# Reciprocal roots of the head norms: GpSimd's power in place of VectorE's Newton steps, in a four-layer conditioned transformer

## The reference, cut to what matters

```python
def _L0_cond_ref(x, c, ...):                     # 16 heads of 18 features
    xn = _ln(x) * (1 + sc_msa) + sh_msa
    q, k, v = heads(xn @ w_qkv + b_qkv)
    q = _ln(q, g_q); k = _ln(k, g_k)             # (q - m) * rsqrt(mean((q - m)**2) + 1e-6) * g
    attn = softmax(q @ k.T * HD ** -0.5)
    x = x + g_msa * ((attn @ v) @ w_proj + b_proj)
    xn2 = _ln(x) * (1 + sc_mlp) + sh_mlp
    return x + g_mlp * (gelu(xn2 @ w1 + b1) @ w2 + b2)
# layer 1: the same without the norms of q and k
# layer 2: the norms of q and k with gain and bias, eps 1e-5
# after it: x + ((x U) R - x U) U^T, R the exponential of a skew matrix made from the condition
```

## Time and profile before

| | us |
|---|---|
| median of 2 runs (4815.79 and 4824.53) | 4820.16 |
| the profiled execution's own time | 4821.86 |
| its span, first to last instruction | 4820.1 |
| PE busy | 4250.8 (88%) |
| DVE busy | 3660.6 (76%) |
| ScalarE busy | 2302.1 (48%) |
| GpSimd busy | 1114.8 (23%) |
| mean granted TensorE clock | 0.943 of full |

### The profile page before, as it was taken

How to read it: one execution, slowest core, us unless ns; L and a number is a source line. 1 busy time by engine, 2 the same in 40 slices (tenths; PEclk the granted TensorE clock), 3 DMA queues, 4 the chain that set the end, 5 groups by cost and what they waited for, 6 DMA issues and landing times. The chain is left out here.

```text
span 4820.1 us, 124616 instructions
## 1 busy us (share of the span) xinstructions
PE 4250.8 (88%) x46073; PEld 3595.5 (75%) x46073; DVE 3660.6 (76%) x7659; ACT 2302.1 (48%) x3894; POOL 1114.8 (23%) x2045
## 2 busy tenths in 40 slices
PE   6754899999999977999999999949989989898998
PEld 4543788888888865888888888737777777777776
DVE  5665889999888845777777777658778787877874
ACT  1212555555555534555555555435454444545443
POOL 1002222222222222222222222212222222222211
PEclk7576999999999988999999999979999999999998
DMA  3001111111111111111111111110010100001000
GB/s 76 21 0 52 32 29 29 29 29 29 29 29 29 27 54 30 30 29 29 29 29 29 29 29 29 37 43 24 20 30 20 28 21 28 21 20 30 20 26 18
DMA packets 122230, 141.59 MB, mean 29 GB/s; under 512 B 14446, under 2 KB 117780, under 8 KB 122112
## 3 DMA queue, kind: packets, MB, share of 16 engines
q1 hardware_dynamic: 121968, 139.75, 10.6%
q10 hardware_dynamic: 144, 0.22, 0.0%
HBM read 110.87 MB, written 29.06 MB: 29 GB/s over the span
## 5 line engine op out<-in xcount | busy, mean ns | idle before, releaser
L869 DVE TENSOR_REDUCE mx<-S 128x4 f32<-128x1024 f32 x768 | 902.7, 1217 | 190.3 <-PE S L1105 187.4
L627 ACT ACTIVATE pT<-S 128x1024 f32<-128x1024 f32 x768 | 745.3, 1023 | 363.2 <-PE S L1133 358.9
L575 ACT ACTIVATE hf<-M 128x512 f32<-128x512 f32 (+1 forms) x480 | 266.2, 555 | 841.8 <-DVE hl L860 597.1
L504 POOL TENSOR_SCALAR hh<-hf 128x512 fp32r<-128x512 f32 (+1 forms) x480 | 286.8, 602 | 1037.2 <-ACT hf L575 1016.4
L1133 PE MATMUL S<-qT,kT 32*128 32x256 f32 x9216 | 427.3, 296 | 65.6 <-ACT pT L627 62.8
L1146 PE MATMUL A<-pT,V 128*32 128x256 f32 x6144 | 416.0, 389 | 26.6 <-ACT pT L627 26.6
L1133 PEld LDWEIGHTS S<-qT,kT 32*128 32x128 f32 x9216 | 330.3, 186 | 138.8 <-ACT pT L627 90.3
L1185 PE MATMUL M<-xh,w_hi 128*128 128x256 f32 x1728 | 365.9, 293 | 3.5 <-POOL xh L480 3.5
L1224 PE MATMUL M<-w_lo,hh 128*128 128x288 f32 x1728 | 351.6, 304 | 0.0
L1185 PE MATMUL M<-xh,w_lo 128*128 128x256 f32 x1728 | 345.0, 281 | 0.0
L1185 PE MATMUL M<-xl,w_hi 128*128 128x256 f32 x1728 | 341.1, 281 | 0.2 <-DVE xm L792 0.2
(11 more groups left out here) (231 smaller groups left out, 9800.8 us busy)
## 6 DMA issues: line engine op xcount, KB each, us to landing
mid<-xbo SPq DMA_DIRECT2D x64, 288.0 KB, 3.2
xld<-mid SPq DMA_DIRECT2D x64, 288.0 KB, 3.0
xa<-mid SPq DMA_DIRECT2D x64, 288.0 KB, 3.6
gA<-gates SPq DMA_DIRECT2D x96, 144.0 KB, 3.3
gM<-gates SPq DMA_DIRECT2D x96, 144.0 KB, 3.0
xld<-in_x_dram SPq DMA_DIRECT2D x32, 288.0 KB, 3.5
xa<-in_x_dram SPq DMA_DIRECT2D x32, 288.0 KB, 3.5
out_dram<-xbo SPq DMA_DIRECT2D x32, 288.0 KB, 2.2
```

The lines of the kernel that those rows point to most:

```text
L504: pool.tensor_scalar(hh[:, 2 * f:2 * f + m, :].rearrange("p m c -> p (m c)"), hf[:, f % 2, 0:m * T], 1.0, 0.0, ALU.mult, ALU.add).then_inc ...
L575: act.activation(hf[:, f % 2, 0:c], MBANK[f % 2][:, 0:c], ACT.Gelu if rot else ACT.Gelu_apprx_tanh).then_inc(s["m_hf"], 1)
L627: act.activation(pT[:, g % 2, 2 * h:2 * h + 2, :], S[:, 2 * h:2 * h + 2, :], ACT.Exp, scale=float(HD) ** -0.5).then_inc(s["a_ex"], 1)
L869: dve.tensor_reduce(mx[:, p, :, :], S[:, r:r + 2, :].rearrange("p a (t k) -> p a t k", t=NT), AX.X, ALU.max).then_inc(s["a_mx"], 1)
```

## The change: what it does

GpSimd gets a new function, `A_heads_rstd`, after the reciprocal root of the layer norm of `nxt` and before the rounding `A_xh`. It waits for the head sums (`a_hs`), makes the mean plus eps in `na` (semaphore `a_hv`) and raises it to -0.5 into `ny` (semaphore `a_hr`). DVE's function of that name, its twelve instructions and their call go; `A_heads_norm` on DVE now first waits for `a_hr`. `mhalf` holds -0.5 and is broadcast along the columns.

```diff
-    a_sq=1, a_hs=1, a_nrm=1, a_v=2, ...
+    a_sq=1, a_hs=1, a_hv=1, a_hr=1, a_nrm=1, a_v=2, ...
...
+                    def A_heads_rstd(n):
+
+                        wait(pool, "a_hs", qk_run(n), 1)
+                        constant_wait(pool)
+                        pool.tensor_scalar(na[:, :], nv[:, :], 1.0 / HD, eps, ALU.mult, ALU.add).then_inc(s["a_hv"], 1)
+                        wait(pool, "a_hv", qk_run(n), 1)
+                        pool.tensor_tensor(ny[:, :], na[:, :], mhalf[:, 0:1].broadcast_to([P, 64]), ALU.pow).then_inc(s["a_hr"], 1)
...
                         if nxt is not None:
                             A_rstd(nxt)
+                        if p is not None and eps is not None:
+                            A_heads_rstd(p)
+                        if nxt is not None:
                             A_xh(nxt)
...
-                    STEPS_P = 0 if eps is None else 14 if rot else 13
+                    STEPS_P = 0 if eps is None else 2 if rot else 1
...
-                    def A_heads_rstd(n):
-
-                        own(dve.tensor_scalar(nv[:, :], nv[:, :], 1.0 / HD, eps, ALU.mult, ALU.add))
-                        own(dve.tensor_scalar(ny[:, :].bitcast(I32), nv[:, :].bitcast(I32), 1, None, ALU.logical_shift_right))
-                        own(dve.tensor_scalar(ny[:, :].bitcast(I32), ny[:, :].bitcast(I32), -1.0, float(NEWTON_MAGIC), ALU.mult, ALU.add))
-                        for _ in range(3):
-                            own(dve.scalar_tensor_tensor(out=na[:, :], in0=ny[:, :], scalar=-0.5, in1=ny[:, :], op0=ALU.mult, op1=ALU.mult))
-                            own(dve.tensor_tensor(na[:, :], na[:, :], nv[:, :], ALU.mult))
-                            own(dve.scalar_tensor_tensor(out=ny[:, :], in0=na[:, :], scalar=1.5, in1=ny[:, :], op0=ALU.add, op1=ALU.mult))
-
                     def A_heads_norm(n, m):
 
+                        wait(dve, "a_hr", qk_run(n), 1)
                         wait(dve, "a_T", n, 0)
...
-                        if p is not None and eps is not None:
-                            A_heads_rstd(p)
                         if d is not None and rot:
                             M_x2(d, 1)
```

More of the change, by code:

```diff
@@ L41 @@
 SQUARINGS, TAYLOR = 9, 6
-NEWTON_MAGIC = 0x5F3759DF
 QK_EPS = (1e-6, None, 1e-5)
@@ L47 @@
     a_x=16, a_g=16, a_st=1, a_ve=1, a_rs=1, a_xn=2, a_xT=2, a_xf=3, a_xh=2, a_xl=1, a_qkv=6, a_qkvd=6,
-    a_sq=1, a_hs=1, a_nrm=1, a_v=2, a_T=4, a_qhi=2, a_khi=2, a_qlo=2, a_klo=2, a_S=8, a_mx=8,
+    a_sq=1, a_hs=1, a_hv=1, a_hr=1, a_nrm=1, a_v=2, a_T=4, a_qhi=2, a_khi=2, a_qlo=2, a_klo=2, a_S=8, a_mx=8,
     a_nm=1, a_nmT=1, a_nmc=1, a_ex=8, a_pv=4, a_o=2, a_oT=2, a_on=4, a_nT=2, a_oh=2, a_ol=2,
```

## The result

The kernel after takes 5151.74 us (median of 2 runs, 5149.75 and 5153.72) against 4820.16 before: ratio 1.069, 95% interval 1.0664 to 1.0715, so 331.6 us slower. The profiled execution took 5153.72 us, with a span of 5152.0. I had forecast 5002, 182 us slower: the sign and the place are as foretold, the size is too small by a factor of 1.8. My forecast's own case reached from 4955 to 5050; the range I gave, 4860 to 5310, holds the time only by what it took in for the rivals, and that is luck.

A forecast was written before the change was run, and what follows sets the result against it. PE bounds the first layer, with Newton 0.9 us off the path; Newton is on the last layer's path. Waiting for a 9.9 us power adds 32 x 3.1 + 32 x 2.6 = 182 us, giving 5002 us, range 4860 to 5310.

The forecast's parts named there:

- What bounds the kernel: Newton on DVE: off the path by 0.9 us in the first layer, on it in the last, worth 2.2 to 2.7.
- Rival 2: GpSimd's power is quick; under 5.0 us the last layer has its full gain, 4747 us, 1.5% faster; chance 0.20.
- The price of the power: Length of GpSimd's power over 64 columns, between 0.85 and 9.9 us; 9.9 taken.
- upper end: GpSimd's power costs 148 ns per further column, as from one column to two, so 9.9 us for 64.
- The wait: DVE's head scaling waits until 10.5 us after the head sums: slots 3.1 us longer in first layer, 2.6 in last.
- GpSimd's own queue: Roundings and V's copies behind the power on GpSimd start late, but their DVE readers are late too: costed at nothing.
- The held port: GpSimd's power holds DVE up as long as it runs: 5207 us, or about 5300; chance 0.25.
- the quick power: GpSimd's power is short and the kernel not slower, down to 4747 us; chance 0.20.
- first threshold: With GpSimd's power under 6.8 us (given as 103 ns a column) the first layer loses nothing.
- The third: GpSimd's power is quick, 5 us, but the port is held against DVE: 4906 us; chance 0.08.
- rival 1: GpSimd's power blocks DVE's two-SBUF-input steps for its whole length: 5207 us, or about 5300; chance 0.25.
- rival 3: GpSimd's power takes 5 us and holds the port, making PE's turn of the next image late: 4906 us; chance 0.08.

The follow-up runs named there:

- no_roots: Kernel after without its power and DVE's wait for it, no Newton steps either, q and k scaled by a constant: 4709.91 us, ratio 0.9783.
- power_40: Kernel after with the power over 40 of the 64 columns, the others left at a constant: 4836.36 us, ratio 1.0042.
- fill_pe: Kernel after with useless transposes on PE in its new idle time, 30 per first-layer slot and 52 per last-layer slot: 5062.73 us, ratio 1.0508.
- mended: Kernel after, first layer's second residual half ahead of the wait; last layer with idle-filling PE transposes and V's copies behind the first hidden-layer rounding: 5008.15 us.
- side_power: Kernel before, Newton steps kept, with the same GpSimd power beside it over constants into a tile nobody reads: 4808.06 us, ratio 0.9979.
- v_late: Kernel after with GpSimd's copies of V moved behind its first rounding of the hidden layer in the last layer: 5151.21 us, ratio 1.0688.

## Why the prediction was right, and where its size was wrong

*What bounds the kernel.* Right for the first layer: Newton is off the path (no_roots: 40.28), with 0.9 of slack (power_40 loses nothing at 7.44). For the last layer Newton is on the path, but its worth was mis-sized: 3.6 a slot, not 2.2 to 2.7, because behind the wait stands DVE's own chain and not only PE's product with V, and because 0.4 of clock comes back with it. Rival 2's 4747 was too modest for that reason; the measured floor is 4710.

*The price of the power.* The upper end was right, and so was the way to it: same operation, more columns. It took 10.6 us rather than 9.9, and DVE went on at 11.22 rather than 10.5. The signals took 0.16 and 0.12 us where I chose 0.15.

*The wait.* Right in mechanism in both layers: M_turn behind the later residual half in the first, the turn of q and k in the last, no cushion in the oraw copy.

*GpSimd's own queue*, costed at nothing. This step failed in the last layer. I asked when the queue's readers need it, and not what it disturbs when it runs: let go by the same event as DVE's scaling, it collides with it, and from the scaling's start to PE's turn it takes 0.8 us more. V's copies, the part that I could move, are worth 0.4 of it at full clock; the two roundings beside the scaling (2.60 us for 1.55) I did not move, so that they make the rest is argued from their place and not shown.

*PE's clock* is missing from the sum altogether. I moved PE's work later by whole microseconds and kept its durations, although each wait that I costed was a stretch with PE idle, and the slot of the earlier trace rows already had the clock at 0.58 and 0.56 behind such a stretch.

*The sum*, per ordinary slot, of which each layer has 27:

| us per slot | first layer | last layer | from |
|---|---|---|---|
| forecast | 3.1 | 2.6 | prediction |
| longer power | 0.7 | 0.7 | 11.22 against 10.5 |
| longer scaling, V's copies being 0.4 of it | - | 0.8 | PE's turn 4.1 late, DVE's start 3.35 |
| PE's clock | 2.2 | 1.0 | after against fill_pe, less the 0.4 of before |
| not placed | -0.2 | -0.2 | what is left |
| measured | 5.8 | 4.9 | after against before |

27 x (5.79 + 4.87) = 288 us; the other 44 fall to the ten slots at the layers' ends, to which I had given 29, most of them to the first two slots of a layer (8.0 and 6.4 us longer in the first layer, 6.6 and 8.6 in the last). Mended takes away the clock and the copies of V, and in the first layer some of the wait itself: 5008 - 4818 = 190 us remain, close to the 182 forecast for the whole, but that is chance, since mended also moved the residual.

*The rivals.* The held port (25%) is excluded by side_power; the quick power (20%) by its 10.6 us, with its first threshold borne out by power_40. Its second is not: at 6.8 us, where 7.3 was to break even, the last layer's slot is 0.3 longer. The third fell with the first. Two of my workings there were wrong: 6.8 us is 99 ns for each column behind the first, not 103; and the forecast, rival 1 and half of rival 3 make 0.76 for slower and leave 0.21 for same, where I put 0.73 and 0.24.

*What stays open:* how much of the last layer's longer scaling comes from each of the two roundings, which parts of the excess in a layer's first slots are wait and which are clock, and why the clock falls in some slots of the kernel before and not in others with the same idle time.

## What to carry to other kernels

When work moves to another engine, ask first how long that engine takes for it and who stands behind the wait in program order: an instruction that needs nothing from the result belongs ahead of the wait. A wait that idles PE for several microseconds can be dearer than its length, so look at the granted clock and the matmuls' durations right behind it. A wait that lets two engines go at once can make them collide; and short steps off the path, or in an idle stretch that can be had by reordering, are cheaper than a handover.

## What the runs showed of the hardware

GpSimd's power over 128 partitions costs 2968, 6813 and 10594 ns at 16, 40 and 64 columns, some 160 ns a column, and does not slow DVE's two-input or one-input steps beside it (side_power). GpSimd's plain copies do: the gain took 1.75 us beside V's copies and 1.50 without them (v_late). In the kernel after, PE came back from 3.88 and 6.47 us of idle time to a granted clock of 0.50 to 0.62 of full for about 4 us, the profile showing 1.00 or 0.81 during the idle time itself. Behind the 2.23 us of the kernel before PE began at full clock, and the clock then fell in 14 of 26 slots. With PE kept busy (fill_pe) it fell in none. Here are the windows of the last layer in the kernel after:

```profile
4059.60:4066.00 6.40, 0.00 (x0) 0.00 (x0) 6.03 (x11) 1.68 (x3) 4.89 (x8) 0.81 0.00 0
4066.00:4068.00 2.00, 1.96 (x9) 1.96 (x10) 1.96 (x4) 0.60 (x1) 0.00 (x0) 0.50 0.00 0
...
4070.00:4072.00 2.00, 2.00 (x18) 2.00 (x17) 1.22 (x4) 0.35 (x1) 0.00 (x0) 0.91 0.00 0
```
